# Graph attention message stages on one Trainium2 core: four tiles' products in one VectorE instruction, and block numbers without a runtime assertion

## What is computed

```python
h = (x @ W).reshape(n, H, D)                    # H*D = 256; H is 4 in layer 0, 8 in layer 1
e = leaky_relu(a_src[src] + a_dst[dst], 0.2)    # one score per edge and head
e = exp(e - segment_max(e, dst)[dst])
alpha = e / segment_sum(e, dst)[dst]
out = segment_sum(alpha[:, :, None] * h[src], dst)
```

## Time and profile before

| | |
|---|---|
| median of 3 runs | 9901.44 us (9900.5 to 9903.71) |
| span of the profiled execution | 12956.2 us |
| PE busy, share of the span | 7687.5 us, 59% |
| DVE busy | 5845.2 us, 45% |
| POOL busy | 5288.2 us, 41% |
| ACT busy | 3553.9 us, 27% |
| message stages in the profile | 691 to 3895 us and 6547 to 9732 us |
| granted TensorE clock, whole span | 0.736 |

### The profile page before, as it was taken

How to read it: one execution, slowest core, us unless ns; L and a number is a source line. 1 busy time by engine, 2 the same in 40 slices (tenths; PEclk the granted TensorE clock), 3 DMA queues, 4 the chain that set the end, 5 groups by cost and what they waited for, 6 DMA issues and landing times. The chain is left out here.

```text
span 12956.2 us, 121430 instructions
## 1 busy us (share of the span) xinstructions
PE 7687.5 (59%) x23227; PEld 4611.4 (36%) x23227; DVE 5845.2 (45%) x17420; ACT 3553.9 (27%) x7703; POOL 5288.2 (41%) x5387
## 2 busy tenths in 40 slices
PE   1345555555459999988645555555555222289994
PEld 1222222222225555544522222222224010056663
DVE  8845555555455333432455555555566000023334
ACT  1123323233333333322323333233335000023323
POOL 0155555555540000032255555555546777700002
PEclk9666666666669999998866666666665555589997
DMA  3133333333331000011433333333343111111117
GB/s 101 62 86 82 82 82 83 81 83 82 81 67 43 15 20 15 18 22 16 98 86 85 85 85 85 83 84 84 83 70 108 13 14 17 12 49 58 56 57 242
DMA packets 570415, 866.54 MB, mean 67 GB/s; under 512 B 203579, under 2 KB 418742, under 8 KB 569482
## 3 DMA queue, kind: packets, MB, share of 16 engines
q0 software_dynamic: 240688, 582.71, 19.0%
q1 hardware_dynamic: 302680, 254.34, 6.4%
q10 hardware_dynamic: 26626, 25.65, 0.6%
HBM read 710.67 MB, written 164.36 MB: 68 GB/s over the span
## 5 line engine op out<-in xcount | busy, mean ns | idle before, releaser
L1307 PE MATMUL g0sm_sump<-k_arena,g0sm_to 128*128 128x260 f32 x3712 | 1587.6, 563 | 1571.4 <-DVE g_acc L1466 948.9
L1307 PE MATMUL g1sm_sump<-k_arena,g1sm_to 128*128 128x264 f32 x3712 | 1623.9, 567 | 1498.0 <-DVE g_acc L1466 929.5
L1203 POOL DMA_INDIRECT k_arena<-htab,g0sm_src x1856 | 1794.2, 967 | 1433.3 <-PE g0sm_sump L1307 834.9
L1203 POOL DMA_INDIRECT k_arena<-htab,g1sm_src x1856 | 1799.7, 970 | 1409.2 <-PE g1sm_sump L1307 840.3
L1452 DVE TENSOR_TENSOR k_arena<-k_arena 128x256 f32<-128x256 f32 x3712 | 1518.9, 410 | 676.2 <-issue 566.2
L1307 PEld LDWEIGHTS g0sm_sump<-k_arena,g0sm_to 128*128 128x128 f32 x3712 | 846.2, 265 | 2259.6 <-issue 1910.4
L1307 PEld LDWEIGHTS g1sm_sump<-k_arena,g1sm_to 128*128 128x128 f32 x3712 | 839.2, 264 | 2227.4 <-issue 1697.1
L794 POOL DMA_INDIRECT re_rerows<-rtab,re_resrc x1024 | 1080.2, 1055 | 326.6 <-issue 326.6
L2472 PE MATMUL f_yp<-k_arena 128*128 128x256 f32 x3136 | 800.0, 401 | 670.3 <-issue 626.7
L1466 DVE TENSOR_TENSOR g_acc<-g_acc,g0sm_sump 128x260 f32 x1856 | 775.2, 418 | 753.6 <-issue 651.8
L2505 DVE TENSOR_TENSOR k_arena<-f_yp,k_arena 128x512 f32<-128x512 f32 x196 | 135.5, 692 | 2123.7 <-remote 1318.8
(11 more groups left out here) (461 smaller groups left out, 8877.4 us busy)
## 6 DMA issues: line engine op xcount, KB each, us to landing
z<-k_arena SPq DMA_DIRECT2D x96, 512.0 KB
k_arena<-z SPq DMA_DIRECT2D x33, 1024.0 KB
k_arena<-htab,g0sm_src POOLq DMA_INDIRECT x1856
k_arena<-htab,g1sm_src POOLq DMA_INDIRECT x1856
x<-g_acc POOLq DMA_DIRECT2D x48, 512.0 KB, 3.4
re_rerows<-rtab,re_resrc POOLq DMA_INDIRECT x1024
cs_zs<-z SPq DMA_DIRECT2D x16, 1024.0 KB
htab<-g1nt_rows POOLq DMA_DIRECT2D x49, 272.0 KB
```

The costliest lines, as they stand in the source:

```text
L1203: nc.gpsimd.indirect_dma_start(slot[a][:, u, :], None, table, bass.IndirectOffsetOnAxis(ap=src[a][:, u:u + 1], axis=0)).then_inc(landed[a] ...
L1307: nc.tensor.matmul(sump[u % BANKS][:, 0:W], to[u // LOT % RING][:, u % LOT, :], slot[a][:, u, 0:W], start=True, stop=True).then_inc(summed, 1)
```

## The change

`messages` replaces `message`: one tensor_tensor of 128x1024 multiplies the features of the four tiles of a lot by their weights, with the weights broadcast along the 256 / H features of a head, and raises `msg_ready` by one for the lot. It stands where the message of the lot's first tile stood; the three others are gone from their rounds. PE waits for `msg_ready` once per lot, beside its wait for the one-hot matrices. `blocks` loads the same values in the same places, with no assertion. The diff, with some unchanged lines left out:

```diff
 def add_up(a, k, u):
     if u % LOT == 0:
         pe.wait_ge(to_ready, k * LOTS + u // LOT + 1)
-    pe.wait_ge(msg_ready, k * T + u + 1)
+        pe.wait_ge(msg_ready, k * LOTS + u // LOT + 1)
     pe.wait_ge(added, k * T + u + 1)
...
 def blocks(a, u, n):
     _, b = nc.values_load_multi_w_load_instructions(
-        blk[a][0:1, u:u + n], engines=[mybir.EngineType.DVE], min_val=0, max_val=NB - 1)
+        blk[a][0:1, u:u + n], engines=[mybir.EngineType.DVE], min_val=0, max_val=NB - 1,
+        skip_runtime_bounds_check_because="edge_layout counts the blocks begun, of 1 to NB, less one")
     return b
-def message(a, k, u):
+def messages(a, k, u):
     if u == 0:
         dve.wait_ge(exp_ready, k + 1)
-    m = slot[a][:, u, 0:DIM].rearrange("p (h d) -> p h d", h=H)
-    tt(m, m, slot[a][:, u, WC].unsqueeze(2).to_broadcast([P, H, D]), ALU.mult).then_inc(msg_ready, 1)
+    m = slot[a][:, u:u + LOT, 0:DIM].rearrange("p t (h d) -> p t h d", h=H)
+    tt(m, m, slot[a][:, u:u + LOT, WC].unsqueeze(3).to_broadcast([P, LOT, H, D]), ALU.mult)\
+        .then_inc(msg_ready, 1)
...
 def both(o, a, k, turn):
     b = blocks(o, HEAD - LEAD, 2 * LOT)
     for s in range(HEAD):
         weigh(s, a, k, turn)
-        message(o, k - 1, HEAD + s)
+        if s % LOT == 0:
+            messages(o, k - 1, HEAD + s)
...
     b = blocks(o, T - LEAD, LOT)
+    messages(a, k, 0)
     for u in range(LEAD):
-        message(a, k, u)
         if u == 1:
             weigh(17, a, k, None)
         add(k - 1, T - LEAD + u, b[u])
     b = blocks(a, 0, 2 * LOT)
     for u in range(LEAD, HEAD):
-        message(a, k, u)
+        if u % LOT == 0:
+            messages(a, k, u)
```

More of the change, by code:

```diff
@@ L1512, in _ @@
                 both(0, 1, N - 1, N // 2 - 1)
-                for u in range(HEAD, T):
-                    message(1, N - 1, u)
+                for u in range(HEAD, T, LOT):
+                    messages(1, N - 1, u)
                 for u in range(HEAD - LEAD, T):
```

## The result

| | before | changed |
|---|---|---|
| median | 9900.97 us (9899.94 to 9903.71, 4 runs) | 10064.17 us (10059.47 to 10066.05, 4 runs) |
| span of the profiled execution | 12956.2 us | 10062.2 us |

The ratio is **1.0162**, 95% interval 1.0151 to 1.0174: the change makes the kernel 163 us slower. The forecast was 10170 us, with a range of 9480 to 10300.

A forecast was written before the change was run, and what follows sets the result against it. POOL's gathers were taken to set the pace, about 40 us per group, with DVE close behind. From 9901 us, 290 us lost to holds and 22 us gained after the last gathers gave 10170 us, range 9480 to 10300.

The forecast's parts named there:

- 3055 us are the profiler's: Whole kernel: the profiled span of 12956 us exceeds the runs' 9901 us only because profiling stretches the execution.
- they shrink by none to 5%: Stretches outside the message stages, 4072 us without the second expert stage's start: 3870 to 4072 us without the profiler.
- The assertion: DVE's block-number loads: the assertion's instructions go, 7.5 us per group taken off DVE, the loads of 595 ns stay.
- the ends: After each call's last gather, DVE finishes about 11 us sooner: 22 us gained over two calls.
- The merged product: DVE's message products: one of about 1.22 us per lot replaces four small ones, saving 1.5 us of DVE per group.
- PE's wait: Semaphores on PE: 24 of 32 waits per group go, a lot's first tile starts up to 1.0 us later; costed at nothing.
- The hold, the step that decides: POOL's gathers starting inside a two-SBUF-input product wait until it is through: 2.5 us more per group, 290 us lost.
- its way of counting starts at random: Hold estimate with gather starts random, 1.25 us apart: a 1.15 us product costs 0.53 us per lot, 4.2 per group.
- DVE sets the pace: Rival, message stages: gathers need less than 1.25 us, DVE's 38 us bounds a group; 9635 us, faster; chance 0.33.
- PE becomes late: Rival: PE's later start, 1.0 us per half group, adds to the holds; 10400 us; chance 0.04.
- nothing on the path: Rival: long products miss POOL's starts or idle time pays for them; 9880 us; chance 0.11.
- The assertion's code stays: Rival, block-number loads: FUSED_REGOPS is needed, only 23 ns per value go; 10170 us as well; no chance of its own.

The follow-up runs named there:

- the four small products: Changed kernel with each lot's merged product as four back-to-back products of 256 elements, PE still waiting once per lot: 9944.94 us, ratio 1.0058.
- the weights in PSUM: Changed kernel with ScalarE writing the exponentials a second time, into PSUM, where the merged product reads its weights: 9740.03 us, ratio 0.9854.
- pairs: Changed kernel with products of two tiles (512 elements), PE waiting per pair: 12645.44 and 12542.80 us, ratios 0.9699 and 0.9701, in the long condition.
- the two others: Kernel without the assertion, PE waiting once per lot: 0.9787 and 0.9820; changed kernel with four small products and weights in PSUM: 0.9831.

## Why the prediction was right, and where it was off

The time fell inside the range and the sign was right; the loss was 163 us where 269 were forecast. The signs that the prediction named came too: the product's line (L1453) stands 928 times, the gathers' means are above 1.03 us, and the longest took 1.97 us.

**What bounds the kernel.** Right: POOL's gathers, one per 1.25 us, set the pace at 9900 us, against what the profile of before showed at first sight. But the argument for it had a false step. "3055 us are the profiler's" is wrong: three jobs timed the same kernel at 12925 to 13048 us. And "they shrink by none to 5%" was too little. What lies outside the gathers is 5003 us; the expert stage with its gathers takes 1400 of it, against the 1341 worked out, as this row of the changed kernel's stretches shows (PE busy 1375 of 1400 us at a clock of 0.99):

```profile
8400.00:9800.00 1400.00, 1375.37 (x4932) 921.63 (x4932) 478.22 (x1538) 429.93 (x598) 999.05 (x1025) 0.99 0.28 65
```

The other stretches have 3600 us instead of 3870 to 4072. So the pace before is 42.0 us per group, not 38.7 to 40.4. The two errors left the right engine in front. That POOL is never idle in the kernel before at 9900 us is inferred, from this budget and from the four other kernels; no profile of it shows it.

**The assertion.** The loads stay at 595 ns and the rest of L1444 is gone, as forecast. Costed at 22 us of gain for both edits at the ends; alone it gave 55. Outside the gathers the kernel with the assertion has 5014 us, those without it 4995 to 5011, so the ends gave 3 to 19 us and the rest is in POOL's pace (42.0 against 4825 / 116 = 41.6 us per group). Its time was off the path as said. That it would change the holds was not foreseen.

**The merged product.** 1215 ns against "about 1.22".

```profile
L1453 DVE TENSOR_TENSOR k_arena<-k_arena x928: 1180/1218/1269, 684.8 to 8163.6; 128x1024 f32<-128x1024 f32 x186
```

DVE was put at 29 us of work and up to 2 of waits; 43.6 less 11.3 for the turned scores is 32. The wait for the exponentials came back as said, 30.8 us in 55 groups, 0.6 us each. So the saving on VectorE was real and worth nothing on the path.

**PE's wait.** Costed at nothing: borne out by the four small products, whose extra time is all in POOL's holds.

**The hold, the step that decides.** The mechanism stands, by the row in the profile after and by the weights in PSUM. Its size was 290 us lost, 268 with the ends; measured are 163, 105 us less. In the changed kernel it is right: 3.2 us of holds per group against 0.8 + 2.5 = 3.3. The scaling behind it holds too between the kernels without the assertion: 2.9 times the 1.1 us of spread products is 3.2. But that 3.3 met 3.2 is partly luck, since the same merged products hold 4.5 us with the assertion in, and nothing in the prediction could tell the two apart.

The term that was mis-sized is the kernel before. All its bounds take off 0.8 us, from a profile where POOL is idle a quarter of the time, though the prediction itself had 1.1 for a POOL that is always at work; and its way of counting starts at random, which gave 4.2 for the long products, gives 32 x 0.335 x 0.335 / (2 x 1.25) = 1.4 for the short ones. The worked-out pace of 42.0 leaves 1.5 us over the 40.9 - 0.35 = 40.5 us that the kernel with the weights in PSUM takes per group without its holds. So a group lost 43.6 - 42.0 = 1.6 us, not 2.5. With the 9901 of the changed kernel's own job the pace is 42.1 and the loss 1.5, 116 x 1.5 = 174 us, less 11 outside the gathers: the result. This sum closes because the pace before is worked out from the times; a profile of that kernel would be the test.

The Trainium skill (SBUF — State Buffer, "SBUF: two separate sides") says that such a VectorE instruction locks out only a GpSimd operation that reads SBUF. The narrow form fits the rows if a gather reads SBUF only at its start: it is held when it starts inside a product, not when a product begins 0.17 us behind its start. What a gather reads there no run shows. "For the whole instruction" is right to within 0.13 us of the product's end.

**The rivals.** "DVE sets the pace" had 0.33. At 9900 us it is out: taking the assertion's 7.5 us per group off VectorE gained 0.5. In the long condition something close to it holds, POOL waits for PE and the change gains; the forecast was for the time shown, so this does not save the rival, but it says that the profile it rested on was a true one of another condition. "PE becomes late" and "nothing on the path" are out. "The assertion's code stays": it does not.

## What to carry to other kernels

Before merging VectorE instructions with two inputs in SBUF, see whether GpSimd issues indirect DMAs beside them and sets the pace: each such instruction held an issue that started inside it until 0.13 us before its end, so the cost grows with the length, not only with the number. Moving one input to PSUM took the hold away and made the merged form a gain (0.985) instead of a loss (1.016). And ask of a profile whose span is not the time of the runs which condition it shows: take durations from it, and the bound only after the budget has been closed against the runs.

## What was not expected of the hardware

- The same kernel took 9880 to 9904 us in two jobs and 12905 to 13062 us in three others, and 12956 us in the profile first shown. In the long condition even stretches without any of the changed code are longer (outside the gathers the changed kernel has 6501 us there, 5003 in the short one), instructions of VectorE and SyncE often start 0.70 us apart (425 and 168 steps of 0.68 to 0.72 us in the changed kernel, against 145 and 2), and the order of the kernels is another: 0.965 for the changed one, 0.970 for pairs, 0.979 to 0.982 and 0.983 for the two others, against 1.016 for the changed one in the short condition. What makes the condition was not found. The four jobs of the experiments ran on four chips, one short and three long, so it may belong to the chip; no chip was used twice.
- Products back to back hold gathers longer than the same products spread, 2.15 against 1.1 us per group, in part because a gather can be held through all four of them.
- A product that starts behind a gather, even by 0.15 us, does not hold it.
- The holds depend on how the two orders fall together: the same merged product holds 4.5 us per group with the assertion in and 3.2 without.
- The assertion makes the instruction traffic of one queue 3.9 times as large. In the page's DMA queues (packets, MB, share of 16 engines), the kernel with merged products and the assertion has

```profile
q14 instruction: 371, 3.04, 0.1%
```

and the changed kernel

```profile
q14 instruction: 95, 0.78, 0.0%
```

The kernel before has 3.06 MB there, the one without the assertion 0.80. No time is known to hang on it.
